# Gated sums, layer norm and top-k attention as one line of sixteen tiles, with no barrier after the experts

## The reference

```python
# second block: 2 of 8 experts for each token
g = a * sigmoid(b)                              # for each expert, width 512
out = out + (g @ Wo.T + bo) * comb[..., e:e+1]
# third block: 77 context rows, 4 heads, the 32 highest scores kept
topv, topi = top_k(scores, 32); probs = softmax(topv)
attn_mean = scatter(probs, topi).mean(heads)    # 77 weights for each token
c_t = attn_mean @ V
x = layernorm(x_text)
scale, shift = split(c_t @ W_film_in + b_film_in)
x = x * (1 + mod_gate * scale) + mod_gate * shift
y = s4d(x, ...)                                 # a long convolution, here by Fourier matrices
```

## Time and profile before

| | before |
|---|---|
| median of 3 runs | 844.28 us (844.15 to 856.82) |
| the profiled execution | 840.17 us, its span 838.1 us |
| PE busy | 677.0 us (81%) |
| DVE busy | 564.4 us (67%) |
| ACT busy | 303.2 us (36%) |
| POOL busy | 389.4 us (46%) |
| last expert matmul ends | 388.69 us into the span |
| barrier after the experts opens | 397.7 us |
| first gated sum transposed on PE | 416.09 us |
| first round of top-k on DVE | 459.29 us |
| barrier after stage C opens | 594.8 us |

### The profile page before, as it was taken

How to read it: one execution, slowest core, us unless ns; L and a number is a source line. 1 busy time by engine, 2 the same in 40 slices (tenths; PEclk the granted TensorE clock), 3 DMA queues, 4 the chain that set the end, 5 groups by cost and what they waited for, 6 DMA issues and landing times.

```text
span 838.1 us, 10777 instructions
## 1 busy us (share of the span) xinstructions
PE 677.0 (81%) x3380; PEld 378.6 (45%) x3380; DVE 564.4 (67%) x1711; ACT 303.2 (36%) x654; POOL 389.4 (46%) x450
## 2 busy tenths in 40 slices
PE   4779698449899999985898568767996999999971
PEld 2434455424354545442486223323442464657651
DVE  4868874667975656510677889988775595744266
ACT  2555564204546555510122535545211311031210
POOL 4979674037887879721102467886200120212020
PEclk9999998559999999988799779978897999999996
DMA  8920011202222222221980000200100000000003
GB/s 223 390 77 1 0 57 36 75 26 77 75 78 75 78 75 77 75 70 38 313 315 25 1 0 2 100 2 1 50 1 0 1 0 1 1 0 1 1 0 100
DMA packets 33087, 52.78 MB, mean 63 GB/s; under 512 B 8718, under 2 KB 21582, under 8 KB 32776
## 3 DMA queue, kind: packets, MB, share of 16 engines
q1 hardware_dynamic: 28040, 36.76, 13.1%
q0 software_dynamic: 4992, 15.34, 5.4%
HBM read 36.62 MB, written 15.47 MB: 62 GB/s over the span
## 4 chain that ended last, share of the span: by engine, by line
PE 44%; DVE 30%; POOL 9%; ACT 7%; issue 6%; DMA 2%; POOLq 1%; SPq 0%; DVEq 0%; ACTq 0%
PE ps L469 40%; DVE arena L1519 5%; DVE arena L2015 4%; POOL arena L1351 3%; DVE arena L2012 3%; POOL arena L1357 2%; DVE arena L335 2%; DVE kp L1519 2%; ACT L1145 1%; DVE arena L1871 1%; DVE arena L1522 1%; DVE arena L1525 1%; DVE arena L1622 1%; ACT arena L988 1%; DVE X L1525 1%
## 5 line engine op out<-in xcount | busy, mean ns | idle before, releaser
L469 PE MATMUL ps<-arena 64*32 64x32 f32 (+10 forms) x2344 | 495.8, 399 | 26.0 <-DVE arena L1808 8.7
L469 PEld LDWEIGHTS ps<-arena 64*32 64x32 f32 (+7 forms) x2344 | 233.7, 155 | 220.0 <-issue 171.4
L988 ACT ACTIVATE arena<-ps 128x512 f32<-128x512 f32 (+4 forms) x252 | 121.1, 493 | 283.3 <-PE ps L469 144.3
L330 POOL TENSOR_SCALAR rstd<-mv 128x1 f32<-128x1 f32 (+2 forms) x30 | 13.0, 434 | 234.4 <-DVE mv L324 183.4
L1871 DVE TENSOR_TENSOR arena<-ps,arena 128x512 f32<-128x512 f32 x39 | 26.9, 689 | 85.4 <-ACT arena L1145 77.4
L1400 POOL DMA_INDIRECT scr_g<-arena,destU x39 | 48.8, 1250 | 44.1 <-DVE arena L1871 35.3
L1391 POOL DMA_INDIRECT arena<-scr_z,idsU x39 | 49.5, 1270 | 22.8 <-PE ps L705 11.5
L2015 DVE MATCH_REPLACE8 arena<-arena 128x77 f32<-128x77 f32 x256 | 54.1, 222 | 0.0
L1145 ACT ACTIVATE arena<-ps 128x512 f32<-128x512 f32 x39 | 23.3, 598 | 83.6 <-PE ps L469 83.5
L1351 POOL TENSOR_TENSOR arena<-arena 128x616 f32<-128x616 f32 x32 | 40.2, 1257 | 20.7 <-DVE arena L1624 19.1
L1283 ACT ACTIVATE arena<-ps,b1p 128x512 f32<-128x512 f32 x32 | 22.0, 687 | 75.9 <-PE ps L469 75.9
(11 more groups left out here) (206 smaller groups left out, 1011.4 us busy)
## 6 DMA issues: line engine op xcount, KB each, us to landing
arena<-in_w1t SPq DMA_DIRECT2D x8, 1024.0 KB, 14.1
arena<-scr_g SPq DMA_DIRECT2D x8, 1024.0 KB, 7.9
X<-in_x SPq DMA_DIRECT2D x2, 1024.0 KB, 6.5
scr_z<-arena SPq DMA_DIRECT2D x4, 512.0 KB, 2.8
arena<-in_c_dftf SPq DMA_DIRECT2D x1, 2048.0 KB, 16.2
arena<-in_L_xattn_W SPq DMA_DIRECT2D x2, 1024.0 KB, 6.3
out<-X SPq DMA_DIRECT2D x16, 128.0 KB, 1.8
scr_k<-arena SPq DMA_DIRECT2D x4, 256.0 KB, 8.2
```

Source lines behind the costliest of these rows:

```text
L469: return pe.matmul(o, l, r, start=first, stop=final)
L988: return a.activation(o, i, ACT.Copy)
```

## The change

- The barrier between stages B and C is gone on all five engines. SP waits only for the scatters before it reads them back; PE waits for the last multiplication and the last kernel copy.
- The memset of `VW` moves to POOL at expert step 27, the bias row's arithmetic to DVE at expert step 36, and its load and the write of the convolution kernel to SP before the end of the experts. The film rows are built in four parts, the last after the first two sums.
- Gated rows are loaded two tiles at a time (16 loads of 512 KB instead of 8 of 1 MB), into eight places.
- The first half of a gated sum (a scaled copy) moves from DVE to ACT (`half_sum`). The product with `wof` has one PSUM bank (4) instead of two, the scores one bank instead of two.
- Only the first seven tiles' sums (`LEAD` = 6) come ahead of top-k; the others stand inside the top-k steps: step n transposes tile n + 7, multiplies tile n + 6 and sums tile n + 8.
- Layer-norm statistics are gathered four tiles at a time; the normalisation of 128x256 moves from DVE to ACT (`norm_u`), with four small POOL operations more for each group.
- The weights: ACT also takes the exponential of the scores that were not taken (`exp_top_and_rest`); POOL subtracts, weighs and adds over heads (`weights`: 4 wide operations instead of 1). DVE's two (L1525 on 128x308, L2036) are gone.
- POOL's `xn` multiplication (L1481) goes into ACT's copy out of PSUM (`put_film`); its 16 additions of a row to `X` (L1483) all stand in steps 8 to 15, two for each.
- On PE the transpose of the weights now stands behind the spectra. The input spectra come in pairs at steps 11 to 14, into two banks, and ACT's two copies of them stand ahead of `exp_top_and_rest`.

```diff
-                stage_end("sync", sp)
+                    sp.wait_ge(s["maskC"], 1)
+                    for b in range(NB):
+                        load(sp, VW[BIAS_ROW:BIAS_ROW + 1, b, :, :].rearrange("p a b -> p (a b)"), d["b_film"], "bfilm_in")
...
+                sp.wait_ge(s["xbA"], 2 * NT)
+                for i in range(2):
+                    sp.wait_ge(s[f"gs{i}"], 16 * ((ST + 1 - i) // 2))
+                def load_gated(i):
+                    for k in range(NSEL):
+                        rowsb = scr_g[(k * NT + 2 * i) * P:(k * NT + 2 * i + 2) * P, :]
+                        load(sp, yg[i][:, k, :, :], rowsb.rearrange("(t p) n -> p t n", p=P), f"gy{i % 4}")
+                load_gated(0)
+                load_gated(1)
                 load_gated(2)
-                sp.wait_ge(s["gy1"], 32)
-                sp.wait_ge(s["sum_ready"], 4)
                 load_gated(3)
                 sp.wait_ge(s["k_out"], 64)
                 load(sp, KL, scr_k.rearrange("(k p) n -> p k n", p=P), "k_in")
                 load(sp, DF, d["c_dftf"].rearrange("(k p) n -> p k n", p=P), "dft_in")
+                for i in (4, 5):
+                    sp.wait_ge(s[f"gy{i - 4}"], 32)
+                    load_gated(i)
+                sp.wait_ge(s["gy3"], 32)
+                load_gated(7)
+                sp.wait_ge(s["gy2"], 32)
+                sp.wait_ge(s["sum_ready"], 8)
+                load_gated(6)
...
-                stage_end("tensor", pe)
...
+                pe.wait_ge(s["g_ready"], ST)
+                pe.wait_ge(s["k_sb"], 2 * KCH)
...
+                def out_B(T):
+                    pe.wait_ge(s["sumT_sb"], T + 1)
+                        pe.wait_ge(s["xB_done"], T)
+                    for f in range(4):
+                        ins = mm(ps[:, 4, 0:D], GT[:, T % 2, f, :], wof[:, f, :], f == 0, f == 3)
...
+                for T in range(LEAD + 1):
+                    turn_sum(T)
+                    if T:
+                        out_B(T - 1)
+                pe.wait_ge(s["prepC_v"], 6)
                 turn_u(0)
                 turn_u(1)
                 scores(0)
...
+                for n in range(NT + 1):
+                    if n + 1 < NT:
+                        scores(n + 1)
+                    if n + LEAD + 1 < NT:
+                        turn_sum(n + LEAD + 1)
+                    if n + LEAD < NT:
+                        out_B(n + LEAD)
+                    if 1 <= n <= 8:
+                        kernel_spectrum(n - 1)
+                    if n == 11:
+                        pe.wait_ge(s["sd_ready"], 2)
+                        pe.wait_ge(s["dfx_in"], 16)
+                        pe.wait_ge(s["ks_done"], 8)
+                    if 11 <= n <= 14:
+                        for i in (2 * (n - 11), 2 * (n - 11) + 1):
+                            if i >= 2:
+                                pe.wait_ge(s["xf_sb"], i - 1)
+                            spectrum(i // 2, i % 2, (5, 4)[i % 2])
+                    if n:
+                        turn_attn(n - 1)
+                    if n + 2 < NT:
+                        turn_u(n + 2)
+                    if n:
+                        film_in(n - 1)
                 stage_end("tensor", pe)
...
+                def half_sum(T):
+                    i = T // 2
+                    a.wait_ge(s[f"gy{i % 4}"], 32 * (i // 4 + 1))
+                    if T >= 2:
+                        a.wait_ge(s["sumT_ps"], T - 1)
+                    a.activation(G[:, T % 2, :], yg[i][:, 0, T % 2, :], ACT.Copy, scale=cw[:, 0, T:T + 1])\
+                        .then_inc(s["gated_half"], 1)
...
+                for T in range(LEAD + 1):
+                    put_sumT(T)
+                    half_sum(T + 2)
+                    if T == LEAD - 1:
+                        norm_u(0)
...
                 for n in range(NT + 1):
                     if n < NT:
+                        exp_all(n)
+                    if n + 1 < NT:
+                        put_scores(n + 1)
+                    if n + LEAD + 1 < NT:
+                        put_sumT(n + LEAD + 1)
+                    if n + LEAD + 3 < NT:
+                        half_sum(n + LEAD + 3)
+                    if 11 <= n <= 14:
+                        put_spectrum(2 * (n - 11))
+                        put_spectrum(2 * (n - 11) + 1)
+                    if n in (2, 6, 10):
+                        norm_u(n // 4 + 1)
+                    if n < NT:
+                        exp_top_and_rest(n)
+                    if 1 <= n <= 8:
+                        put_kernel(n - 1)
                     if n:
+                        put_attn(n - 1)
+                    if n + 2 < NT:
+                        put_uT(n + 2)
+                    if n:
+                        put_film(n - 1)
...
+                def weights(n):
+                    q_, E = smC[:, n % 2], Ex[:, n % 2, :]
+                    p.wait_ge(s["ex_sum"], n + 1)
+                    own.done(p.tensor_tensor(q_[:, 1, :], q_[:, 0, :], negone[:], ALU.pow))
+                    own.settle()
+                    own.done(p.tensor_scalar(q_[:, 2, :], q_[:, 1, :], tmask[:, n:n + 1], None, ALU.mult))
+                    p.wait_ge(s["rest_exp"], n + 1)
+                    own.done(p.tensor_tensor(E, E, Rk[:, n % 2, :], ALU.subtract))
+                    own.settle()
+                    hE = E.rearrange("p (h k) -> p h k", h=H1)
+                    own.done(p.tensor_tensor(hE, hE, q_[:, 2, :].unsqueeze(2).broadcast_to([P, H1, S2]), ALU.mult))
+                    own.settle()
+                    own.done(p.tensor_tensor(E[:, 0:2 * S2], E[:, 0:2 * S2], E[:, 2 * S2:SW], ALU.add))
+                    own.settle()
+                    if n >= 2:
+                        p.wait_ge(s["AT_ps"], n - 1)
+                    p.tensor_tensor(a77[:, n % 2, :], E[:, 0:S2], E[:, S2:2 * S2], ALU.add).then_inc(s["attn_ready"], 1)
...
+                for n in range(NT + 2):
+                    if n in (2, 6, 10):
+                        rstd_u(n // 4 + 1)
+                    if n >= 2:
+                        x_in(n - 2)
+                    if 1 <= n <= NT:
+                        weights(n - 1)
...
+                    if TB <= n < NT:
+                        for T in (2 * (n - TB), 2 * (n - TB) + 1):
+                            p.wait_ge(s["u_ready"], T + 1)
+                            p.tensor_tensor(X[:, T, :], X[:, T, :], rows[:, BNO, :], ALU.add).then_inc(s["xbE"], 1)
...
+                for T in range(LEAD):
+                    sum_gated(T + 2)
+                    add_B(T)
+                for n in range(NT):
+                    top_eight(n, 0)
+                    top_eight(n, 1)
+                    if n + LEAD + 2 < NT:
+                        sum_gated(n + LEAD + 2)
+                    top_eight(n, 2)
+                    if 2 <= n <= 9:
+                        kernel_pair(n - 2)
+                    top_eight(n, 3)
+                    if n + LEAD < NT:
+                        add_B(n + LEAD)
                 v.wait_ge(s["ks_done"], 8)
...
```

More of the change, by code:

```diff
@@ L241, in build @@
         a77 = rc.take(2, S2)
-        xn = rc.take(2, D)
+        filmT = rc.take(2, D)[:, 0, :]
+        nmrC = rc.take(NT)
         KL = rc.take(L // P, D)
@@ L1193, in put_scores, with exp_all @@
+                    a.activation(Sc[:, n % 2, :], bank(2, SW), ACT.Copy, scale=1.0 / math.sqrt(DH1))\
                         .then_inc(s["sC_read"], 1)
+                def exp_all(n):
+                    a.wait_ge(s["top_neg"], n + 1)
+                    if n >= 2:
+                        a.wait_ge(s["attn_ready"], n - 1)
+                    for h in range(H1):
+                        a.activation(Ex[:, n % 2, h * S2:(h + 1) * S2], Sc[:, n % 2, h * S2:(h + 1) * S2], ACT.Exp,
+                                     bias=smC[:, n % 2, 3, h:h + 1])
@@ L1199, in _ @@
+                half_sum(0)
+                half_sum(1)
+                for b in range(NB):
+                    for g in range(2):
+                        a.wait_ge(s["prepC_ps"], 8 + 2 * b + g)
+                        copy(wqk[:, g, b, :], bank((4, 5, 1, 7)[2 * b + g], SW)).then_inc(s["prepC_sb"], 1)
+                for T in range(LEAD + 1):
[3 more added lines that the diff above has]
+                        norm_u(0)
                 put_uT(0)
@@ L1305, in _ @@
             own.done(p.memset(onesb[:], 1.0))
-            own.done(p.memset(onerow[:], 1.0))
             own.done(p.memset(halfpi[:], math.pi / 2))
@@ L2020, in _ @@
[L2020 to L2037 removed]
+                            v.wait_ge(s["attn_ready"], n - 1)
```

483 lines of the change are left out of this document (204 added, 279 removed).

## The result

| | before | after |
|---|---|---|
| median of 20 runs | 844.65 us (840.28 to 856.82) | 858.73 us (847.76 to 873.60) |
| the profiled execution | 840.17 us, span 838.1 | 848.9 us, span 847.1 |
| last expert matmul ends | 388.69 us | 394.44 us |
| then: first gated sum transposed | +27.4 | +12.7 |
| then: top-k begins on DVE | +70.6 | +34.0 |

The account below looks back on a forecast made before the run. DVE was taken to bound stage C's window, busy 119.3 of 135.6 us. Saving 36 us before top-k and giving back 28 in it ends the stage 8.8 us earlier: median 835.5 us, 8-in-10 range 820 to 849.

Parts of the forecast that it names:

- Part 1: Stage C up to top-k: without the barrier and with seven tiles instead of sixteen, 36 us are saved.
- part 2: Top-k itself: each engine's step added up anew, 28 us given back, about 163 us instead of 135.6.
- steps 1 to 8: First half of top-k: PE's 8.6 us plus a stall of some 0.4 bounds each step, seven steps at 9.1.
- POOL's weights: POOL in each top-k step: one power, subtraction, weighing and adding over heads, 4.0 us together.
- a sign against part 2: POOL in top-k: the top-k forecast is wrong if POOL's two new wide passes differ from 0.7 us.
- Rival D: POOL in top-k: passes take twice DVE's, 7 to 14 us more, 846 us; chance 0.08.
- 4.7 us of the barrier are waiting for nothing that the loads need: Barrier between stages B and C: last scatter lands at 393.0, loads start at 397.8, so 4.7 us are needless.
- three steps at 9.2 and 8.2 for the last: Last third of top-k, after tile 11: ACT's loop sets three steps at 9.2 us, the last takes 8.2.
- 0.5 to 1 for each ... 3.5 in all: PE's gaps in top-k: lower clock adds 0.5 to 1 us each where PE is on the loop, 3.5 in all.
- stages D to F are as before: Behind stage C: these stages were to take the same time as in the kernel before.
- The two loops: Top-k: POOL's order makes at least 8.2 us a step, ACT's order 9.2 us in steps 11 to 14.

Follow-up runs that it names:

- the first experiment: POOL's drain taken out of the end of stage C, against the kernel after: 830.62 us, ratio 0.996 to before, 6.2 us below after.

## Why the prediction was wrong

**What was right.** Part 1, counted from the last expert matmul: SP's first load forecast at +4.4 and issued at +4.5, the first transpose of a sum at +13.8 and +12.7, top-k at +34.3 and +34.0 (+35.4 in one repetition). In part 2 the spectrum of the first full step ended at +51.8, and the transpose behind it stands at +51.8. The steps 1 to 8 were to take 9.1 and took 8.96 on the mean, with PE as the bound and a stall of 0.31 us where 0.4 was given. POOL's weights were put at 4.0 us and measure 1.04 + 0.31 + 0.84 + 0.70 + 0.46 + 0.32 with small gaps, 3.95: the subtraction is longer than the 0.70 it was given, which the prediction had named as a sign against part 2, but the sum holds. The transpose of tile 10's weights was due at +145.8 and stands at +144.8. Rival D, with POOL's passes at twice DVE's, is out: 0.84 and 0.70 us for 308 columns, against the 1.07 it put. DVE's pass of that width, of another kind, took 0.53. The Trainium skill (GPSIMD Engine Reference, section 3.1 on elementwise work) has a ratio of 1.96 for an addition of 2048 columns; at the width of 308 here the trace shows 1.6 and 1.3.

**The steps that failed.** Together they carry the profiled execution from the forecast 831.4 to 848.9. The change was to gain 8.8 us and costs some 5, so 14 us have to be found, and the first two rows are 11.3 of them:

| step of the prediction | forecast | measured | difference |
|---|---|---|---|
| "4.7 us of the barrier are waiting for nothing that the loads need": the drain is saved | 0 at C's end | 6.5 between POOL's last operation and PE | +6.5 |
| "three steps at 9.2 and 8.2 for the last" and "0.5 to 1 for each ... 3.5 in all" for the clock | last operation +197.3 | +202.1 | +4.8 |
| (not named) experts end as before | 388.7 | 394.4 | +5.7 |
| "stages D to F are as before" | 243.2 | 244.0 | +0.8 |

The table's 17.8 and the 17.5 between the two executions differ by what lies around the span. The other 5.7 us of the 23.2 between forecast and median are no step of the kernel: the median of after stands 9.8 us above its profiled execution, where the prediction added the 4.1 of before.

*The drain.* The prediction read 7.65 us on POOL's end of stage, saw the last scatter land 2.7 us after its issue, and took the difference for a wait that the barrier forces and that goes with it. The reading of the landing was right, and so was that nobody needs the wait. What it did not ask is what POOL's drain waits for if not the scatters, and whether the next drain would be short because the stage before had paid. The pair of runs, the drain taken out of after's C (stage C 6.2 us shorter) and out of before's B alone (stage C 2.9 us longer), shows that it is owed once. No rival of the prediction had it.

*The last third.* Top-k as a whole, due at 163 us, took 168.1 up to POOL's last operation and 174.6 up to where PE goes on. Up to tile 11 the transposes of the weights are within 1.1 us of the forecast. The two loops were found and rightly ordered; the term that was mis-sized is the clock, 3.5 us for all gaps together. The forecast's sum at full clock puts POOL's last operation at +194.0, and it ended 8.1 us later, 4.8 above the sum *with* the 3.5. By steps: the period that ends with tile 11 took 10.2 us instead of 8.2, for the 12 instructions of scores and spectra in it took 7.43 us at a granted clock of 0.63; the next three took 10.8, 10.7 and 11.0 instead of 9.2, of which 1.6 each is the same 12 at 6.43 instead of 4.86 us behind a gap of 2.73 us; the last took 9.3 instead of 8.2 and the tail 5.3 instead of 4.2, with PE standing 6.4 us ahead of each transpose and its film product at 2.08 instead of 1.13 us. The prediction had the rows for it. Behind a gap of 2.5 us six instructions took 4.07 us instead of 2.74; this is the gap:

```profile
577.56 0.50 PE L818 MATMUL ps<-ident,arena 128*77 128x128 f32 x1 [2.50 <-DVE arena L2036]
```

Counted once for each of these steps, those 1.3 us come near the 1.6 measured; the prediction gave "0.5 to 1".

*The experts.* The profiled executions of before end them at 388.7 and 395.4, those of after at 394.4 and 390.4 us. No step of the change explains that, and one pair of profiles can't be read to better than these 5 us without a mark inside the kernel to count from.

*Stages D to F.* They start with 32 multiplications of one column. In the timeline of PE after:

```profile
603.08 6.99 PE L480 MATMUL ps<-gb_ffn,arena 128*128 128x1 f32 x32 [8.90 <-POOLq L321]
```

and in that of before:

```profile
594.85 4.52 PE L469 MATMUL ps<-gb_ffn,arena 128*128 128x1 f32 x32 [0.72 <-ACTq L315]
```

They take 2.5 us more. The long gap, and with it the drain, is not needed for that: without the drain at C's end, in the first experiment, the gap is 2.5 us and they are as slow. (A gap can do it by itself: in the kernel before without the drain at B's end, 6.95 us stand ahead of them and they take 6.99 too.)

```profile
582.83 6.99 PE L480 MATMUL ps<-gb_ffn,arena 128*128 128x1 f32 x32 [2.51 <-POOLq L1587]
```

What goes with it is TensorE's clock ahead of them: in the kernel after the granted clock is 0.50 from 585.0 us on, where PE is busy for 2.6 of 18.1 us, and in the kernel before it is 0.88 in the last 9.9 us of stage C, where PE is busy for 8.5. From the end of stage C to the end of the span the profiles of after are 0.8 to 2.9 us longer than those of before.

**What stays open.** In the two pairs of profiles stage C and what follows are 3.2 and 7.3 us longer after the change (0.4 and 0.9%); in the second, 1.4 us of it stand ahead of top-k, where the first product with `wof` took 3.51 us instead of 1.99. Why the stages behind C take up to 246.2 us in some profiles and 244.0 in others, no run shows. Open too is what POOL's first drain after the experts does in its 7.2 us; between the first drain (1.15 us) and this one lie POOL's 78 indirect DMAs, which fits, but no run took them away.

## What to carry to other kernels

Before a barrier is taken out, look at what every engine's drain in it costs, and where its next drain stands: a cost that is owed once moves to the next one, and if that is at an exposed end the gain is lost. When work is spread into a steady loop, write down for each engine which of its instructions stand between a result and the one that waits for it; what turned this change from 0.5% slower into 2.5% faster was not less work but one drain left out and two such orders changed, the largest of the three being POOL doing the urgent product before the late one. And where a wait of 2 to 3 us stands ahead of long multiplications on PE, count the price of the lower clock that a row of the old trace shows, once for each step.

## What the runs showed of the hardware

- POOL's first drain after the experts' gathers and scatters took 7.2 to 7.65 us in all profiles that have one, whether right behind the last of them or 200 us later; all other drains of POOL took 0.83 or 1.15. With a report by semaphore after POOL's own last instruction in its place, PE went on 0.13 us after that instruction (+202.0 and +202.1) and 6.2 us earlier.
- Behind a gap of 2.73 us on PE 12 instructions took 6.43 us at a granted clock of 0.73, between the two levels of 0.50 and 1.00. In the runs with gaps of 1.35 and of 1.48 us in their place they took 4.86 (at 1.00) and 4.74 us.
- POOL needs 0.84 us for a subtraction of 308 columns and 0.70 for a multiplication of the same width by a factor repeated along the row.
